# FFN tiles between the last attention outputs, and weight maxima spread through memory instead of GpSimd

## The reference

```python
x = x + attn_a(layernorm(x))   # 32 heads of 128, 8 key/value heads, int4 codes * scales, rope, causal
x = x + ffn(layernorm(x))      # 8 experts, the 2 best by the gate; y = x @ A[e].T @ B[e].T, rank 64
x = x + attn_b(layernorm(x))   # 32 heads of 16, 8 key/value heads, rope, causal, f32 weights
x = x + ffn(layernorm(x))      # the same weights once more
```

## Time and profile before

| | |
|---|---|
| median of 3 runs | 1042.6 us (1042.29 to 1045.12) |
| profiled execution | 1044.38 us |
| its span, first to last instruction | 1042.5 us |
| granted TensorE clock, mean | 0.975 |
| PE busy | 965.8 us, 93% |
| DVE busy | 804.2 us, 77% |
| ACT busy | 620.6 us, 60% |
| POOL busy | 580.4 us, 56% |

### The profile page before, as it was taken

How to read it: one execution, slowest core, us unless ns; L and a number is a source line. 1 busy time by engine, 2 the same in 40 slices (tenths; PEclk the granted TensorE clock), 3 DMA queues, 4 the chain that set the end, 5 groups by cost and what they waited for, 6 DMA issues and landing times.

```text
span 1042.5 us, 21597 instructions
## 1 busy us (share of the span) xinstructions
PE 965.8 (93%) x7715; PEld 533.3 (51%) x7715; DVE 804.2 (77%) x1869; ACT 620.6 (60%) x1362; POOL 580.4 (56%) x570
## 2 busy tenths in 40 slices
PE   3698999999999999999999999689987799998998
PEld 1244555555555555555555555345555455554554
DVE  5877887887887887887887888767867888882744
ACT  2267666666666666666666655444377488886131
POOL 3768876876886876876876873143655011110111
PEclk9989999999999999999999999899999699999999
DMA  8164475374475374475374374400000000000002
GB/s 288 48 194 123 87 198 132 76 197 131 77 197 131 76 197 131 77 191 133 81 197 131 77 158 137 91 1 2 1 1 2 1 2 3 3 2 2 1 1 81
DMA packets 179895, 95.48 MB, mean 92 GB/s; under 512 B 168032, under 2 KB 168544, under 8 KB 175200
## 3 DMA queue, kind: packets, MB, share of 16 engines
q1 hardware_dynamic: 170016, 49.64, 22.1%
q10 hardware_dynamic: 9792, 44.59, 13.2%
HBM read 50.17 MB, written 2.10 MB: 50 GB/s over the span
## 4 chain that ended last, share of the span: by engine, by line
PE 74%; DVE 9%; POOL 5%; ACT 5%; issue 5%; DMA 1%; SPq 0%; ACTq 0%; DVEq 0%; POOLq 0%
PE bank L986 14%; PE bank L987 14%; PE bank L988 14%; PE bank L1386 4%; PE bank L1073 3%; PE bank L1075 3%; PE bank L1074 3%; PE bank L1093 3%; PE bank L1095 3%; PE bank L1094 3%; PE bank L1329 2%; PE bank L1310 2%; PE bank L1334 2%; PE bank L1295 1%; DVE bank L1584 1%
## 5 line engine op out<-in xcount | busy, mean ns | idle before, releaser
L501 POOL TENSOR_TENSOR rt<-rt 128x512 f32<-128x512 f32 x80 | 101.1, 1267 | 137.9 <-DVE rt L1569 137.9
L1601 DVE SCALAR_TENSOR_TENSOR bw_hi<-bank,rden,bw_hi 128x128 f16<-128x128 f32 (+3 forms) x256 | 123.3, 544 | 61.4 <-ACT bw_hi L765 61.4
L734 ACT ACTIVATE bank<-bank,shift,c_score 128x128 f32<-128x128 f32 (+3 forms) x256 | 147.3, 605 | 2.1
L1584 DVE CUSTOM_DVE_ANT_0 bank<-bank,mask_w 128x512 f32<-128x512 f32 (+3 forms) x256 | 118.1, 520 | 21.6 <-PE bank L1075 21.3
L765 ACT ACTIVATE bw_hi<-bank,rden 128x128 f16<-128x128 f32 (+3 forms) x256 | 114.5, 536 | 25.3 <-DVE rden L1594 25.2
L729 ACT ACTIVATE shift<-smax,c_score 128x4 f32<-128x4 f32 x64 | 19.0, 297 | 163.4 <-DVE smax L1584 163.4
L986 PE MATMUL bank<-xt,wq_hi 128*128 128x512 f16 x256 | 99.2, 387 | 2.2 <-DVE rt L1569 1.8
L746 ACT ACTIVATE pt<-bank,c_score_b 128x512 f32<-128x512 f32 x128 | 81.1, 686 | 29.7 <-PE bank L1295 29.7
L987 PE MATMUL bank<-xt,wq_hi 128*128 128x512 f16 x256 | 98.7, 385 | 0.0
L988 PE MATMUL bank<-xt,wq_lo 128*128 128x512 f16 x256 | 98.5, 385 | 0.0
L986 PE MATMUL bank<-wo_hi,arena 128*128 128x512 f16 x256 | 97.5, 381 | 0.6 <-DVE x L1613 0.6
(11 more groups left out here) (234 smaller groups left out, 2619.6 us busy)
## 6 DMA issues: line engine op xcount, KB each, us to landing
qcode<-in_q_codes ACTq DMA_DIRECT2D x8, 1024.0 KB, 5.0
qscale<-in_q_scales ACTq DMA_DIRECT2D x8, 1024.0 KB, 8.0
ocode<-in_o_codes ACTq DMA_DIRECT2D x7, 1024.0 KB, 4.9
oscale<-in_o_scales ACTq DMA_DIRECT2D x7, 1024.0 KB, 8.8
kvcode<-in_k_codes ACTq DMA_DIRECT2D x8, 256.0 KB, 8.7
kvcode<-in_v_codes ACTq DMA_DIRECT2D x8, 256.0 KB, 9.0
kvscale<-in_k_scales ACTq DMA_DIRECT2D x8, 256.0 KB, 8.9
kvscale<-in_v_scales ACTq DMA_DIRECT2D x8, 256.0 KB, 9.2
```

Source lines behind the costliest of these rows:

```text
L734: act.activation(a_rows(i, s), a_rows(i, s), ACT.Exp, bias=shift[:, s % 2, c:c + 1], scale=c_score[:, 0:1], accum_out=bank[3][:, SUMS_AT + ...
L1584: dve.tensor_tensor_reduce(bank[bk][:, o:o + (i + 1) * P], bank[bk][:, o:o + (i + 1) * P], mask_w[:, S - (i + 1) * P:S], 1.0, LOWEST, ALU. ...
L1601: dve.scalar_tensor_tensor(out=p_row[:, s % 2, LO_AT[i]:LO_AT[i] + P_STEP * i + 1:P_STEP], in0=turned_back(i, s), scalar=rden[:, s % 2, c: ...
```

## The change

On PE the list behind the last group becomes: output tile 3, context 6, two norm transposes, the first tile's gate and lora_a, context 7, the second tile's, output tiles 4 and 5 with transposes, the third tile's, output tile 6, the fourth tile's, output tile 7; then `experts(0, HALF)` for tiles 4 to 7. DVE and ACT get the matching order. `first` holds what was the body of the loop; the banks of the first FFN's two gate halves are exchanged.

The maxima of a lot no longer go through POOL. SP stores the three columns in a DRAM tensor and reads them back into every partition, in the memory of `m_turned`, and DVE reduces 3 x 128 values. `w_largest` stands one head earlier in the last group; `w_factors(0)` moves from head 7 to head 5, and ACT scales and splits lora_a and the gate inside the last group and lora_b between FFN tiles. Lot 1's maxima come two tiles later and its factors after the gate of the first FFN, at which point SP spreads them; its scaling on ACT goes wholly to the second stage. POOL writes the low halves in smaller pieces between the variance powers.

The diff, cut to the changed lines:

```diff
@@ -95,7 +95,7 @@
 HALF = NT // 2
-GATE_BANK = [5, 7]
+GATE_BANK = [(7, 5), (5, 7)]
@@ -349,10 +349,13 @@
+        largest_of = [nc.dram_tensor(f"largest{lot}", (P * 3,), F32).ap() for lot in range(2)]
+        largest_all = m_turned[:].rearrange("p i n -> p (i n)").bitcast(F32)[:, 0:3 * P]
...
         d_x = [sem(f"d_x{t}") for t in range(ST)] + [sem("d_x_rest")]
-        d_raw, amaxw_done, redw, invw_done = ([sem(f"{n}{i}") for i in range(2)] for n in (
-            "d_raw", "amaxw_done", "redw", "invw_done"))
+        d_raw, amaxw_done, d_largest, d_spread, redw, invw_done = ([sem(f"{n}{i}") for i in range(2)] for n in (
+            "d_raw", "amaxw_done", "d_largest", "d_spread", "redw", "invw_done"))
@@ -440,9 +443,21 @@
+            def spread(lot):
+                sp.wait_ge(amaxw_done[lot], 3)
+                sp.dma_start(largest_of[lot].rearrange("(p c) -> p c", c=3), amax_w[:, 3 * lot:3 * lot + 3]
+                             ).then_inc(d_largest[lot], 16)
+                sp.wait_ge(d_largest[lot], 16)
+                sp.dma_start(largest_all, largest_of[lot].partition_broadcast(P)).then_inc(d_spread[lot], 16)
...
                 for s in range(8):
+                    if (j, s) == (KV_HEADS - 1, 4):
+                        spread(0)
                     turn_head(j, s, j == 0)
+            spread(1)
@@ -579,13 +594,6 @@
-            def largest(lot):
-                c = slice(lot * 3, lot * 3 + 3)
-                pool.wait_ge(amaxw_done[lot], 3)
-                pool.partition_all_reduce(pow_w[:, c], amax_w[:, c], P, bass.bass_isa.ReduceOp.max
-                                          ).then_inc(redw[lot], 1)
@@ -593,15 +601,14 @@
-            largest(0)
+            for part in range(4):
+                w_low("lora_a", part, 4)
+            w_low("gate", 0, 1)
...
                 ln_rsqrt(1, t)
-            w_low("lora_a", 0, 1)
-            w_low("gate", 0, 1)
-            between = {2 + i: ("b_q", i, 4) for i in range(4)}
-            between.update({6 + i: ("b_kv", i, 2) for i in range(2)})
+            between = {4 + i: ("b_q", i, 4) for i in range(4)}
@@ -619,20 +626,22 @@
             for t in range(ST, NT):
+                w_low("lora_b", t - ST, 4)
                 ln_rsqrt(1, t)
-            w_low("lora_b", 0, 1)
-            largest(1)
-            pool.wait_ge(wlo_done, 3)
+            pool.wait_ge(wlo_done, 9)
...
             pool.memset(bv[:, :, KV_HEADS * B_VD:], 0.0).then_inc(zeros_done, 1)
+            pool.wait_ge(o_ps, NT * KV_HEADS)
             weighted(0)
-            w_low("b_o", 0, 1)
+            for part in range(2):
+                w_low("b_kv", part, 2)
             for t in range(NT):
+                if t < 4:
+                    w_low("b_o", t, 4)
@@ -792,6 +801,16 @@
+            def w_scale(n):
+                i = WEIGHTS.index(n)
+                act.wait_ge(invw_done[i // 3], 1)
+                act.activation(raw[n], raw[n], ACT.Copy, scale=inv_w[:, i:i + 1]).then_inc(w_scaled, 1)
+            def w_high(n):
+                act.wait_ge(w_scaled, WEIGHTS.index(n) + 1)
+                act.activation(w_hi[n][:], raw[n], ACT.Copy).then_inc(whi_done, 1)
@@ -838,10 +857,16 @@
...
                 rope_hi(j, ("q", 7))
+                if last:
+                    w_scale("lora_a")
+                    w_high("lora_a")
...
                 probs_high(j, 6)
+                if last:
+                    w_scale("gate")
+                    w_high("gate")
@@ -863,21 +888,6 @@
...
             ctx_high(KV_HEADS - 1, "cc", 6)
-            ctx_high(KV_HEADS - 1, "cc", 7)
-            def w_scale(n):
-                i = WEIGHTS.index(n)
-                act.wait_ge(invw_done[i // 3], 1)
-                act.activation(raw[n], raw[n], ACT.Copy, scale=inv_w[:, i:i + 1]).then_inc(w_scaled, 1)
-            def w_high(n):
-                act.wait_ge(w_scaled, WEIGHTS.index(n) + 1)
-                act.activation(w_hi[n][:], raw[n], ACT.Copy).then_inc(whi_done, 1)
-            for n in LOTS[0]:
-                w_scale(n)
-                w_high(n)
@@ -891,27 +901,41 @@
+            def h_out(ph, t):
+                act.wait_ge(h_ps, NT * ph + t + 1)
+                act.activation(hidden[:, t], bank[t % 2][:], ACT.Copy).then_inc(h_done, 1)
...
                 m0 = ph * 2 * NT
-                ln_hi(c, 0)
-                for t in range(NT):
+                if ph == 0:
+                    ln_hi(c, 0)
+                    ln_hi(c, 1)
+                    h_out(ph, 0)
+                    ctx_high(KV_HEADS - 1, "cc", 7)
+                    h_out(ph, 1)
+                    ln_hi(c, 2)
+                    w_scale("lora_b")
+                    ln_hi(c, 3)
+                    h_out(ph, 2)
+                    w_high("lora_b")
+                    h_out(ph, 3)
+                    ln_hi(c, 4)
+                else:
+                    ln_hi(c, 0)
+                for t in range(HALF if ph == 0 else 0, NT):
...
                         gate_exp(ph, 1)
-                    act.wait_ge(h_ps, NT * ph + t + 1)
-                    act.activation(hidden[:, t], bank[t % 2][:], ACT.Copy).then_inc(h_done, 1)
+                    h_out(ph, t)
...
                         gate_exp(ph, 0)
-                    if ph == 0 and HALF < t < NT - 1:
-                        w, n = beside[t - HALF - 1]
-                        w(n)
...
                     m_high(m0 + t, PROJ_DN_B)
-                    if ph == 0 and t < 5:
-                        w, n = beside[t + 1]
+                    if ph == 0 and t < 7:
+                        w, n = beside[t - 1]
@@ -1176,10 +1200,6 @@
...
             group(KV_HEADS - 1, 1, "last")
-            a_pv(KV_HEADS - 1, "cc", 6, KV_HEADS, "tail")
-            a_pv(KV_HEADS - 1, "cc", 7, KV_HEADS, "tail")
-            for t in range(ST - 1, NT):
-                a_out(KV_HEADS - 1, 1, "oo", t, KV_HEADS, "tail")
@@ -1212,26 +1232,26 @@
-            def experts(ph):
+            def first(ph, t):
+                c = 1 + 2 * ph
+                pe.wait_ge(xt_done, NT * c + t + 1)
+                e0 = t % HALF * EXPERTS
+                wide(bank[GATE_BANK[ph][t // HALF]][:, e0:e0 + EXPERTS], t, "gate", EXPERTS).then_inc(g_ps, 1)
+                if t == NT - 1:
+                    turn(ph * 2 * NT, hs[:, 0], hs_done, ph * NT + 1)
+                if t >= 2:
+                    pe.wait_ge(h_done, ph * NT + t - 1)
+                wide(bank[t % 2][:], t, "lora_a", D).then_inc(h_ps, 1)
+            def experts(ph, t0):
...
                 m0, f0 = ph * 2 * NT, ph * NT
-                if ph == 0:
-                    ln_t(c, 0)
-                if ph == 0:
-                    pe.wait_ge(wlo_done, 2)
-                for t in range(NT):
+                for t in range(t0, NT):
...
                         ln_t(c, t + 1)
-                    pe.wait_ge(xt_done, NT * c + t + 1)
-                    e0 = t % HALF * EXPERTS
-                    wide(bank[GATE_BANK[t // HALF]][:, e0:e0 + EXPERTS], t, "gate", EXPERTS).then_inc(g_ps, 1)
-                    if t == NT - 1:
-                        turn(m0, hs[:, 0], hs_done, f0 + 1)
-                    if t >= 2:
-                        pe.wait_ge(h_done, f0 + t - 1)
-                    wide(bank[t % 2][:], t, "lora_a", D).then_inc(h_ps, 1)
+                    first(ph, t)
                 if ph == 0:
-                    pe.wait_ge(wlo_done, 3)
+                    pe.wait_ge(wlo_done, 9)
@@ -1241,7 +1261,29 @@
-            experts(0)
+            j = KV_HEADS - 1
+            a_out(j, 1, "oo", 3, KV_HEADS, "tail")
+            a_pv(j, "cc", 6, KV_HEADS, "tail")
+            pe.wait_ge(plo_done, 32 * KV_HEADS)
+            ln_t(1, 0)
+            ln_t(1, 1)
+            pe.wait_ge(wlo_done, 5)
+            pe.wait_ge(o_added, NT * j + 3)
+            first(0, 0)
+            a_pv(j, "cc", 7, KV_HEADS, "tail")
+            first(0, 1)
+            ln_t(1, 2)
+            a_out(j, 1, "oo", 4, KV_HEADS, "tail")
+            ln_t(1, 3)
+            a_out(j, 1, "oo", 5, KV_HEADS, "tail")
+            first(0, 2)
+            a_out(j, 1, "oo", 6, KV_HEADS, "tail")
+            first(0, 3)
+            a_out(j, 1, "oo", 7, KV_HEADS, "tail")
+            ln_t(1, 4)
+            pe.wait_ge(o_added, NT * j + 7)
+            experts(0, HALF)
@@ -1267,7 +1309,7 @@
-            pe.wait_ge(wlo_done, 3 + 4 + 2 + 1)
+            pe.wait_ge(wlo_done, 9 + 4 + 2)
@@ -1442,14 +1484,17 @@
...
                 second(NT + t, "b_o")
-            experts(1)
+            experts(1, 0)
-            def power_of_two(value, inv, c, red, done):
+            def power_of_two(value, inv, c, spread_done, red, done):
+                dve.wait_ge(spread_done, 16)
+                dve.tensor_reduce(value[:, c], largest_all.rearrange("q (p c) -> q c p", c=3), AX, ALU.max
+                                  ).then_inc(red, 1)
@@ -1625,7 +1670,8 @@
-                power_of_two(pow_w, inv_w, slice(3 * lot, 3 * lot + 3), redw[lot], invw_done[lot])
```

(57 more changed lines are left out.)

## The result

The changed kernel takes 1047.65 us (median; 1044.2 to 1050.43), the kernel before 1043.74 beside it (1039.92 to 1046.46): ratio 1.0041, 95% interval 1.0031 to 1.0052. It is slower by about 4 us; 1040.9 was forecast, within 1036.3 to 1044.8. A gap, in what follows, is idle time of TensorE.

The account below looks back on a forecast made before the run. TensorE was taken to bound the kernel, losing 15.0 us between output tile 2 and the first lora_b tile; -5.1 + 1.0 + 1.4 + 1.0 (clock) = -1.7 us gave 1040.9 us, range 1036.3 to 1044.8.

Parts of the forecast that it names:

- part 3: lora_b stage and lot 1's factors: second lora_b tile +1.0 us, end of the stage +1.4 us.
- I take 2.0 to 2.7 each, nearest to the stores: Lot 1's spread before the second lora_b tile: store and read-back each take 2.0 to 2.7 us, queues being empty.
- rival B: Lot 1's spread decides: at 4.7 us a transfer, factors come 4.8 late, kernel +3.1 us, 1045.7; chance 0.09.
- signs of being wrong: Gate matmul waiting for POOL; DVE over 1 us at a factor-step DMA; clock below 1 after 682; first lora_b outside 719 to 725.
- I had 1.0 for both late places: Clock falls after 681.4 and in the lora_b stage: +1.0 us for the two together, within 0 and 5.4.
- Part 1: Last group, to output tile 2: +2.5 us, from lot 0's factors on DVE and lora_a's scaling on ACT.
- Part 2: Output tile 2 to the first lora_b tile: 15.0 us of TensorE loss become 7.4.
- Part 3, powers: End of the lora_b stage: norm 2's powers between b_o's quarters delay TensorE by +1.4 us, from 0 to +2.

Follow-up runs that it names:

- experiment 1: Changed kernel with 14 filler matmuls on TensorE ahead of the second lora_b tile; ratio 1.0013 to the kernel before.
- run 2: Changed kernel with lot 1's factors behind the first y_add, b_q's scale and high half later, norm 2's powers ahead of b_o's quarters; ratio 0.9999.
- run 4: Changed kernel with lot 1's maxima spread by the all-reduce on POOL again, behind its third product with the gate weights; ratio 1.0076.
- run 6: Changed kernel with context 6 put ahead of output tile 3 on TensorE; ratio 1.0039.
- experiment 7: Changed kernel with lot 1's maxima in DVE's earlier idle times and its factors where the kernel before has them; ratio 0.9984.
- experiment 8: Kernel of experiment 7 plus norm 2's powers ahead of b_o's quarters, context 6 ahead of output tile 3, sel ahead of lora_b's low quarters; 1040.41 us, ratio 0.9965.
- experiment 9: Changed kernel with only POOL's m_stack memset and sel moved ahead of lora_b's low quarters; ratio 1.0019.
- experiment 3: Changed kernel with only norm 2's powers for tiles 0 to 3 moved ahead of b_o's quarters on POOL; ratio 1.0019.
- experiment 5: Kernel before with only the spread of both lots' maxima changed, to two transfers and a DVE reduction; ratio 1.0012.

## Why the prediction was wrong

**The step that failed** is in part 3, "I take 2.0 to 2.7 each, nearest to the stores". The rest of that step held: the last maximum ends 2.35 us ahead of the first lora_b tile (2.4 forecast), DVE is done with the gate 1.9 behind it (1.2 to 2.2 forecast). The two transfers measured 2.57 and 3.73, 6.3 in all and not 4.0 to 5.4, 3.15 each on average. The rows gave 2.0 for stores alone; a chain of store and read back to 128 partitions was not in them, and the mean of my two ends (3.35) would have been nearer than the row that looked nearest. ("DMA: Bandwidth & Descriptors" of the Trainium skill, section "Anatomy of one DMA", gives about 2.0 us of fixed cost, measured for transfers that GpSimd issues; these are SP's, and the trace shows 2.57 for 1.5 KB.) By rival B's own rule ("from 2.4 us a transfer on") 3.15 each adds 2 x 0.75 = 1.5 to the 5.1 between the tiles: 6.6, measured 6.82. B's mechanism came, at a third of its price. Two of the prediction's own signs of being wrong are in the trace: DVE stood 2.11 us at a transfer at the second factor step, and the granted clock was below 1 after 682 (0.50 in 732 to 736).

**The clock took the price up.** I took a gap of about 2.1 there to be like the 2.25 of the earlier trace rows, after which nothing fell; no run has such a gap in this place. At 3.63 the clock fell, for 12 matmuls at 0.43: 2.6 us, and 3.0 by experiment 1. I had 1.0 for both late places. There was a fall ahead of the first gate tile as well (0.67 in 676 to 680): in runs 2, 4, 6, 7 and 8 that stretch kept its clock and the tile starts 79.9 after the load of lora_a, in after 80.5. The 0.6 are not saved there, for in those runs the clock falls behind that tile instead, and run 2 reaches the first lora_b tile 1.1 later than after.

**Part 1** held: +2.60 for +2.5, the gap before head 6's second score 3.59 for 3.4 to 3.5. The clock fell behind that gap too (0.50 in 658 to 660), but ACT's high half of lora_a, over at 661.17, came later than DVE's maximum (660.24) and set head 6's exponentials, so the fall was hidden.

**Part 2** held in its mechanism and its gaps (3.19 for 3.25, 1.22 and a slow clock for 2.4, 1.70 for 1.75; context 7 waited for no transpose) and lacked two terms: sel beside the norm of tile 7, 1.4 to 1.6 (experiment 9), and the clock. -5.2 for -7.6. I had the row that tells it, 3.83 for 0.54 beside a POOL subtraction, and used it for lora_b's end only; POOL, freed of the all-reduce, starts sel 0.3 us behind the memset in front of it (711.29 and 711.56), where it was 7.2 (713.04 and 720.21), right into DVE's norm. In the kernel before, sel ran beside no norm; DVE was mostly idle then (1.85 ahead of 721.57).

**Part 3, powers**: 1.8 for 1.4 (experiment 3), right in kind.

**The sum**: +2.6 - 5.2 + 2.8 + 4.5 = +4.7, against a forecast of -1.7: 6.4 more. Of these 1.8 come from the spread, 2.2 from the clock (2.6 + 0.6, less the 1.0 forecast), 0.5 from the powers and hand-offs, 1.8 from part 2 (sel, small waits) and 0.1 from part 1.

**The root** lies behind the step that failed. The transfer's length shows because the change also moved lot 1's maxima behind the fourth tile, from 14.3 to 2.35 us ahead of the first lora_b tile. With the maxima early and transfer and tile order as in the change, the 2.1 us wait, the gap and the clock's fall are all gone (experiment 7, which also moves the factors ahead of the second gate half, as the early maxima allow). The late maxima can be lived with if the factors are late too: experiment 2, which also moves the powers, is level with the kernel before. What experiment 5 adds is that the transfer is no shorter anywhere, so an early maximum, or a late use, is the condition for it. I had read the maxima's new place as a given, and asked only how long the transfer behind them would take.

**Open**: theory 4, a cost of the tile order as such, was not tried with the order alone taken back. In experiment 8, which has it, the stretch from output tile 2 to the first lora_b tile is 4.8 us shorter than before, so with the maxima early parts 1 and 2 together pay.

## What to carry to other kernels

When a reduction is turned into a transfer, move its input to the front: the time from the last input to the first use has to cover store, read and the use's own queue, and DVE's idle times of 3 to 5 us in the stretch before are the place for it. Price a gap with the clock behind it, and at the gap's high end rather than its middle: here the gap was 3.63 in place of 2.1, and 2.6 us of slow matmuls came behind it. And when an engine is freed, look at what it will do sooner, and beside whom.

## What the runs showed of the hardware that I had not expected

- A store of 1.5 KB from 128 partitions and a read of 192 KB back to them took 2.57 and 3.73 us in after, with no other transfer of the kernel in flight. For lot 1's spread the other runs have 2.3 to 3.1 for the store and 3.0 to 4.0 for the read, 5.7 to 6.4 together; the 256 KB stores take 2.0.
- The clock and gaps: TensorE resumed at 1.2 GHz behind the gaps of 3.63 (after), 3.46 (run 3) and 3.41 (run 9); behind 3.30 (run 6) the matmuls slowed after 1.4 us of work, behind 3.22 (run 4) the whole tile ran at full speed, as behind 2.25. In order of these gaps 12, 12, 8, 6 and 0 of the tile's twelve matmuls were slow. Other gaps of 2.3 ahead of the first gate tile had a fall behind them (0.57 in 684 to 688 in run 2), and the same code had it in two places (after and run 2), so one gap's length doesn't tell it alone.
- One partition_all_reduce kept POOL for 12.6 us with 0.38 recorded (experiment 4): 5.52 ahead of the record and 6.68 behind it. The part ahead was hidden in the kernel before where POOL came to the reduce well ahead of its input; the 6.79 of the earlier trace rows stands behind it there too.
- The strided reduction of 3 x 128 values on DVE takes 0.65 to 0.68 us, between the bounds of 0.16 and 2.28, and above the scaled 0.43.
